# A decoder layer with 64 experts: the experts' token rows gathered in four pieces and turned by VectorE

## The reference

```python
x = x + attention(layernorm(x))            # causal, 16 heads, x is 4 x 1024 x 1024, float32
x = x + cross_mix(layernorm(x), ctx)
h = layernorm(x); probs = softmax(h @ gate.T)          # 64 experts
top_val, top_idx = top_k(probs, 8)                     # 8 experts for each token
# experts chosen only as 5th to 8th are replaced by a similar one (similarity >= 0.5)
for each expert: y = (silu(h[tok] @ Wg.T) * (h[tok] @ Wu.T)) @ Wd.T    # 384 wide
x = x + sum over experts of y * weight
```

## Time and profile before

| | |
|---|---|
| median of 3 runs | 7594.9 us (7593.01 to 7607.1) |
| span of the profiled execution | 7591.9 us |
| TensorE busy, whole span | 93% |
| expert stage, 3601.17 to 7591.9 us: TensorE, DVE, ACT, POOL busy | 3971, 1851, 1636, 1300 us of 3991 |
| DMA engines busy there | 59% |

### The profile page before, as it was taken

The page is one execution under the profiler, slowest core; times in us unless marked ns, Lnnn a source line. Parts: engine busy times, 40 slices in busy tenths (PEclk is TensorE's granted clock), DMA queues, the critical chain, the costliest instruction groups (busy, mean ns, idle before and its releaser), DMA issues.

```text
span 7591.9 us, 118507 instructions
## 1 busy us (share of the span) xinstructions
PE 7089.7 (93%) x37743; PEld 5849.8 (77%) x37744; DVE 3948.7 (52%) x7056; ACT 3419.9 (45%) x6382; POOL 1810.6 (24%) x1602
## 2 busy tenths in 40 slices
PE   7998998998995999992999999999999999999999
PEld 5777777777774787872888888888888888888887
DVE  5666666667664344336454444444444444444444
ACT  4666666666664122211344444444444444444443
POOL 1122122122110000000333333333333333333333
PEclk9999999999997999995999999999999999999999
DMA  2222222222212222221565555665555565566555
GB/s 73 55 66 59 54 65 62 54 64 62 55 50 82 84 64 75 78 70 32 157 182 155 156 159 159 168 180 160 161 163 161 160 166 160 161 163 170 159 158 151
DMA packets 313829, 875.34 MB, mean 115 GB/s; under 512 B 44128, under 2 KB 85600, under 8 KB 313568
## 3 DMA queue, kind: packets, MB, share of 16 engines
q0 software_dynamic: 98928, 365.58, 20.7%
q1 hardware_dynamic: 214640, 506.45, 20.6%
HBM read 614.84 MB, written 206.70 MB: 108 GB/s over the span
## 4 chain that ended last, share of the span: by engine, by line
PE 52%; DVE 0%; DMA 0%; POOL 0%; issue 0%; ACT 0%; DVEq 0%; POOLq 0%; ACTq 0%
PE ps_gu L1928 10%; PE ps_gu L1930 10%; PE ps_gu L1929 10%; PE ps_y L1928 5%; PE ps_y L1930 5%; PE ps_y L1929 5%; PE ps_xe L1948 3%; PE ps_xe L1957 1%; PE ps_l L1937 1%; PE ps_h L2040 0%; DVE logits L2202 0%; DMA out<-y_sup,scatter_s 0%; DMA x_rows<-rows,gather_s 0%; DVE xs_lo L2248 0%; DVE at_hi L2195 0%
## 5 line engine op out<-in xcount | busy, mean ns | idle before, releaser
L1928 PE MATMUL ps_gu<-xs_hi,gu_hi 128*128 128x512 f32 x3072 | 1213.5, 395 | 7.3 <-DVE gu_lo L2287 7.3
L1930 PE MATMUL ps_gu<-xs_hi,gu_lo 128*128 128x512 f32 x3072 | 1207.7, 393 | 0.0
L1929 PE MATMUL ps_gu<-xs_lo,gu_hi 128*128 128x512 f32 x3072 | 1204.8, 392 | 0.0
L1907 POOL TENSOR_TENSOR dn_lo<-raw_w,dn_hi 128x512 fp32r<-128x512 f32 x384 | 485.1, 1300 | 945.3 <-ACT dn_hi L2110 945.3
L1928 PEld LDWEIGHTS ps_gu<-xs_hi,gu_hi 128*128 128x128 f32 x3072 | 578.0, 188 | 130.6 <-DVE gu_lo L2287 7.7
L1929 PEld LDWEIGHTS ps_gu<-xs_lo,gu_hi 128*128 128x128 f32 x3072 | 578.2, 188 | 125.2
L1930 PEld LDWEIGHTS ps_gu<-xs_hi,gu_lo 128*128 128x128 f32 x3072 | 577.7, 188 | 125.0
L454 PE MATMUL ps_qkv<-xt_hi,w_hi 128*128 128x512 f32 x1512 | 619.6, 410 | 17.6 <-ACT proj L610 9.9
L1928 PE MATMUL ps_y<-dn_hi,hs_hi 128*128 128x512 f32 x1536 | 628.6, 409 | 0.1
L889 DVE TENSOR_TENSOR pt_lo<-ps_t,pt_hi 128x512 fp32r<-128x512 f32 (+3 forms) x768 | 425.4, 554 | 376.3 <-ACT pt_hi L710 371.6
L454 PE MATMUL ps_qkv<-xt_lo,w_hi 128*128 128x512 f32 x1512 | 609.7, 403 | 0.0
(11 more groups left out here) (325 smaller groups left out, 15534.7 us busy)
## 6 DMA issues: line engine op xcount, KB each, us to landing
raw_w<-w_gu SPq DMA_DIRECT2D x384, 512.0 KB, 4.1
raw_w<-w_down SPq DMA_DIRECT2D x192, 512.0 KB, 6.5
w_raw<-wqkv SPq DMA_DIRECT2D x192, 256.0 KB, 2.6
turned<-proj SPq DMA_DIRECT2D x512, 64.0 KB, 2.0
out<-residual SPq DMA_DIRECT2D x36, 512.0 KB, 2.6
q_hi<-q_hi SPq DMA_DIRECT2D x128, 128.0 KB, 2.3
attn_out<-out_t POOLq DMA_DIRECT2D x128, 128.0 KB, 2.3
residual<-x SPq DMA_DIRECT2D x32, 512.0 KB, 4.6
```

What stands on the lines that cost most here:

```text
L1907: pool.tensor_tensor(dn_lo[:, f, a], raw_w[:, f, a], raw(dn_hi[:, f, a]), ALU.subtract).then_inc(dn_lo_ok, 1)
L1928: pe.matmul(out, a_hi, w_hi, start=first, stop=False)
L1929: pe.matmul(out, a_hi, w_lo, start=False, stop=False)
L1930: return pe.matmul(out, a_lo, w_hi, start=False, stop=last)
```

## The change

In `rows` a token is now four pieces of 256 features, each followed by 64 columns; the routing weights stand in the first piece, and zeros in the other three. One gather of 128 rows becomes four of 128 pieces: the gather for slot `q` brings pieces such that partitions 32j to 32j+31 hold the j-th quarter of the features of 32 tokens. DVE then turns all 32 x 32 squares of such a block in place with one instruction (`turn_super`, `turn_tail` on DVE), and the features are on partitions. TensorE's turns and `ps_xe` are gone. ACT and DVE split a block with one instruction of 1024 elements instead of two of 512, and DVE's now reads SBUF twice where one input was in PSUM. The host lays the first layer's weights out in the same order of features.

The list of row numbers of an expert is written into one of four slots of a ring (`table`), and 16 further instructions on 32 partitions each write the numbers of the pieces (`pieces`). The three first gathers of an expert's blocks are issued one expert earlier, behind the `send_super` of the same number; the fourth stays where all four were.

```diff
-                sp.dma_start(rows[row:row + P, 0:H], work[:, 1, :]).then_inc(x3_out, 16)
+                sp.dma_start(rows[row:row + P, :, 0:QF], work[:, 1, :].rearrange("p (q c) -> p q c", q=Q4)).then_inc(x3_out, 16)
...
-                sp.dma_start(rows[a, 0:H], res[:, 0, :]).then_inc(zero_out, 16)
-                sp.dma_start(rows[a, H:H + E], res[:, 0, 0:E]).then_inc(zero_out, 16)
+                sp.dma_start(rows[a, :, 0:QF], res[:, 0, :].rearrange("p (q c) -> p q c", q=Q4)).then_inc(zero_out, 16)
                 sp.dma_start(out[a, :], res[:, 0, :]).then_inc(zero_out, 16)
...
+            for q in range(Q4):
+                sp.dma_start(rows[:, q, QF:ROW].rearrange("(n p) e -> p n e", p=P),
+                             blank[:, :].unsqueeze(1).broadcast_to([P, SUP + N, E])).then_inc(blank_out, 16)
...
-        xt_lo = m.sb("xtail_lo", [P, H], F32R)
+        xt_hi = m.sb("xtail_hi", [P, HB, P], F32R)
+        xt_lo = m.sb("xtail_lo", [P, HB, P], F32R)
         act_s = m.sb("act_s", [P, TOKENS])
         hs_hi = m.sb("hs_hi", [P, FB, TOKENS], F32R)
         hs_lo = m.sb("hs_lo", [P, FB, TOKENS], F32R)
@@ -1752,11 +1761,12 @@
...
+            pieces_of_rows = rows.rearrange("n q c -> (n q) c")
             def gather_super(n, i):
-                if i == 0:
-                    pool.wait_ge(gs_ok, START + n + 1)
-                    pool.wait_ge(wn_ok, START + n)
-                    pool.wait_ge(xs_ps, START + n * SUP)
-                    stand_alone(pool, passed)
-                pool.indirect_dma_start(x_rows[:, i, 0:H + E], None, rows,
-                                        bass.IndirectOffsetOnAxis(ap=gather_s[:, i:i + 1], axis=0)).then_inc(rows_s[i], 16)
+                pool.wait_ge(gs_ok, START + n + 1)
+                pool.wait_ge(wn_ok, START + n)
+                if not (isinstance(n, int) and n == 0):
+                    pool.wait_ge(xs_lo_ok, START + (n - 1) * SUP + i + 1)
+                stand_alone(pool, passed)
+                for q in range(Q4):
+                    pool.indirect_dma_start(x_rows[:, i, q, 0:ROW], None, pieces_of_rows,
+                                            bass.IndirectOffsetOnAxis(ap=gather_s[:, i * Q4 + q:i * Q4 + q + 1], axis=0)).then_inc(rows_s[i], 16)
             def gather_tail(n):
                 pool.wait_ge(gt_ok, START + n + 1)
                 pool.wait_ge(wtn_ok, START + n)
-                pool.wait_ge(xt_ps, START + n)
+                pool.wait_ge(xt_lo_ok, START + n)
                 stand_alone(pool, passed)
-                pool.indirect_dma_start(xt_rows[:, 0:H + E], None, rows,
-                                        bass.IndirectOffsetOnAxis(ap=gather_t[:, 0:1], axis=0)).then_inc(rows_t, 16)
+                for q in range(Q4):
+                    pool.indirect_dma_start(xt_rows[:, q, 0:ROW], None, pieces_of_rows,
+                                            bass.IndirectOffsetOnAxis(ap=gather_t[:, q:q + 1], axis=0)).then_inc(rows_t, 16)
...
             for i in range(SUP):
                 gather_super(0, i)
+            for i in range(SUP - 1):
+                gather_super(1, i)
             def super_block(e, t0, t1):
                 send_last(e + t0)
                 gather_tail(e + t0)
-                for i in range(SUP):
-                    gather_super(e + 1, i)
+                gather_super(e + 1, SUP - 1)
                 for n in range(2 * FB):
                     pool.wait_ge(hi_ok, START + e * 2 * CHUNKS + 2 * GUC + n + 1)
                     f, a = n // 2, slice(n % 2 * BANK, (n % 2 + 1) * BANK)
                     pool.tensor_tensor(dn_lo[:, f, a], raw_w[:, f, a], raw(dn_hi[:, f, a]), ALU.subtract).then_inc(dn_lo_ok, 1)
                 for i in range(SUP - 1):
                     send_super(e, t0, i)
-            def tail_block(e, t):
+                    gather_super(e + 2, i)
+            def tail_block(e, t, t0):
                 gather_tail(e + 1 + t)
                 send_last(e + 1 + t)
...
-            def turn_super(n, i, tails):
-                pe.wait_ge(rows_s[i], (n + 1) * 16)
-                pe.wait_ge(xt_lo_ok, START + tails * 2)
-                pe.wait_ge(xs_lo_ok, START + n * 2 * SUP + 2 * i)
-                for k in range(HB):
-                    mm = pe.transpose(ps_x1[:, k * P:(k + 1) * P], x_rows[:, i, k * P:(k + 1) * P], ident[:, :])
-                mm.then_inc(xs_ps, 1)
...
-                turn_tail(e + t0, e + 1)
                 first_layer(2, 0)
                 first_layer(2, 1)
-                turn_super(e + 1, 0, e + 1 + t0)
...
                 for i in range(1, SUP):
-                    turn_super(e + 1, i, e + 1 + t0)
                     for c in range(2):
...
                 turn_h(1)
-                turn_tail(e + 1 + t, e + 2)
                 turn_h(2)
...
             def split_super(n, i):
...
+                act.wait_ge(xs_turned, START + n * SUP + i + 1)
...
                 act.wait_ge(up_ok, START + n * FB)
-                for c in range(2):
-                    ks = slice(c * GQ, (c + 1) * GQ)
-                    act.activation(xs_hi[:, ks, i * P:(i + 1) * P],
-                                   ps_x1[:, c * BANK:(c + 1) * BANK].rearrange("p (k c) -> p k c", c=P), ACT.Copy).then_inc(xs_hi_ok, 1)
+                act.activation(by_feature(xs_hi[:, :, i * P:(i + 1) * P]), in_order(x_rows[:, i, :, :]), ACT.Copy).then_inc(xs_hi_ok, 1)
             def split_tail(n, t):
-                act.wait_ge(xt_ps, START + n + 1)
...
-                    split_super(e + 1, i)
-                    if i < SUP - 1:
-                        finish(i)
-            def tail_block(e, t):
+                split_super(e + 1, 0)
+                split_super(e + 1, 1)
+                finish(0)
+                split_super(e + 1, 2)
+                split_super(e + 1, 3)
+                finish(1)
+                finish(2)
...
-                at = tails_before(dve, n) + n * SUP
-                dve.tensor_tensor(table[:, bass.ds(at + 1, N)], found[:, 0, :], found[:, 1, :], ALU.add).then_inc(list_ok, 1)
+                at = (n & AHEAD) * N
+                dve.tensor_tensor(found[:, 0, :], found[:, 0, :], found[:, 1, :], ALU.add).then_inc(total_ok, 1)
+                dve.wait_ge(total_ok, START + n + 1)
+                stand_alone(dve, passed)
+                dve.tensor_copy(table[:, bass.ds(at, N)], found[:, 0, :])
+                mine = pieces[:, bass.ds(at * Q4, N * Q4)].rearrange("p (n i) -> p n i", i=Q4)
+                for q in range(Q4):
+                    for i in range(Q4):
+                        ins = dve.tensor_scalar(mine[32 * q:32 * q + 32, :, i], found[32 * i:32 * i + 32, 0, :], float(Q4), float(q), ALU.mult, ALU.add)
+                ins.then_inc(list_ok, 1)
...
-                dve.tensor_copy(gather_s[:, :], table[:, bass.ds(n * SUP + tails + 1, SUP)]).then_inc(gs_ok, 1)
+                dve.tensor_copy(gather_s[:, :], pieces[:, bass.ds((n & AHEAD) * N * Q4, SUP * Q4)]).then_inc(gs_ok, 1)
...
+                dve.tensor_copy(gather_t[:, :], pieces[:, bass.ds(at * Q4, Q4)]).then_inc(gt_ok, 1)
+            def turn_super(n, i):
+                dve.wait_ge(rows_s[i], (n + 1) * 64)
+                dve.transpose(x_rows[:, i, :, 0:QF], x_rows[:, i, :, 0:QF]).then_inc(xs_turned, 1)
+            def turn_tail(n):
+                dve.wait_ge(rows_t, LOADED + (n + 1) * 64)
+                dve.transpose(xt_rows[:, :, 0:QF], xt_rows[:, :, 0:QF]).then_inc(xt_turned, 1)
...
             def rest_of_super(n, i):
-                for c in range(2):
-                    dve.wait_ge(xs_hi_ok, START + n * 2 * SUP + 2 * i + c + 1)
-                    a = slice(i * P, (i + 1) * P)
-                    ks = slice(c * GQ, (c + 1) * GQ)
-                    dve.tensor_tensor(xs_lo[:, ks, a], ps_x1[:, c * BANK:(c + 1) * BANK].rearrange("p (k c) -> p k c", c=P),
-                                      raw(xs_hi[:, ks, a]), ALU.subtract).then_inc(xs_lo_ok, 1)
+                dve.wait_ge(xs_hi_ok, START + n * SUP + i + 1)
+                a = slice(i * P, (i + 1) * P)
+                dve.tensor_tensor(by_feature(xs_lo[:, :, a]), in_order(x_rows[:, i, :, :]), raw(by_feature(xs_hi[:, :, a])),
+                                  ALU.subtract).then_inc(xs_lo_ok, 1)
...
-                dve.tensor_copy(w_next[:, :], x_rows[:, :, bass.ds(n + H, 1)].rearrange("p i a -> p (i a)")).then_inc(wn_ok, 1)
+                for i in range(Q4):
+                    ins = dve.tensor_copy(w_next[32 * i:32 * i + 32, :], x_rows[0:32, :, i, bass.ds(n + QF, 1)].rearrange("p s a -> p (s a)"))
+                ins.then_inc(wn_ok, 1)
...
             make_list(0)
             finish_list(0)
-            gather_super_index(0, 0)
+            gather_super_index(0)
             make_list(1)
+            turn_super(0, 0)
+            for i in range(SUP):
+                if i + 1 < SUP:
+                    turn_super(0, i + 1)
+                rest_of_super(0, i)
             keep_weights(0)
```

(19 more changed lines are left out.)

120 lines of the change are left out of this document (58 added, 62 removed).

## The result

The changed kernel takes 8393.8 us (median of 4 runs, 8354.8 to 8417.5), the kernel before 7599.1 us beside it: a ratio of 1.1042 (95% interval 1.1013 to 1.1072), 10% slower. The direction of the forecast was right, its size was not: 7837 was forecast, and 8060 was the upper end.

A forecast was written before the change was run, and what follows sets the result against it. The prediction took TensorE to bound the expert stage (busy 3971 of 3991 us). Its terms, -282 + 179 + 279 + 51 + 15 = +242 on 7591.9, plus 3.0 to the median, gave 7837 us, range 7555 to 8060.

The forecast's parts named there:

- term 3: Tail: POOL's scatters and 12 gathers make the tail's rows late, delaying the next expert's first product; +279 us.
- At nothing: Effects charged zero: mixing-stage stores, ACT's saved instructions, and gathers with 18% more bytes, four times the packets, queues having room.
- Term 1: Transposes removed from TensorE: 320 turns of eight in dense streams at 0.88 us each save 282 us.
- Term 2: Second layer: DVE is 3.2 us late for multiply(2), so TensorE waits 2.8 us in each expert; +179 us.
- The turn: DVE's 128 x 1024 transpose instruction, taken as 1.2 us; a skill-based estimate gave 2.5 us.
- Term 4: End of the second layer: results leave ps_y late, 0.8 us in each of 64 experts; +51 us.
- Term 5: Start: sixteen gathers instead of four ahead of the first expert, and three lists with 16 pieces each; +15 us.
- A gather of pieces is cheap: Faster rival: on POOL, a gather step below 0.71 us removes term 3, 7558 us; deciding point 0.79 us; chance 0.13.
- DVE is later still: Slower rival: DVE's lateness for multiply(2) costs 5.5 us an expert in Term 2, giving 8008 us; chance 0.22.

The follow-up runs named there:

- e1: The changed kernel with one gather of 128 whole rows in place of four gathers of pieces, same bytes, rows not rightly placed: 7780.3 us, ratio 1.0241.
- e3: The changed kernel with DVE's order alone changed: finish_list last in super_block, turn_super(3) behind rest_of_h(2): 7953.5 us, ratio 1.0469.
- e7: The changed kernel with e1 and e3 together, one gather for a block and finish_list last: 7473.9 us, ratio 0.9845.
- e11: The changed kernel with all its work in another order on POOL and DVE, gathers in shorter runs, one finish of ACT moved: 8088.2 us, ratio 1.0651.
- e4: The kernel before with each gather of 128 rows made four gathers of 128 quarter rows at the same place: 8559.4 us, ratio 1.1259.
- e14: e13 with one wait changed: POOL starts the gathers of blocks 1 and 2 when hs_lo of f = 0 is written: 7571.0 us, ratio 0.9969.
- e8: The kernel before with two gathers of half rows in place of each gather, at the same place: 7861.3 us, ratio 1.0348.
- e9: e4 with three of every four gathers replaced by a direct DMA of the same 128 x 1,088 bytes, issued by POOL: 7597.0 us, ratio 1.0002.
- e10: The kernel before with 15 memsets of 128 x 1024 on POOL behind the five gathers, no further DMA: 7595.2 us, ratio 0.9995.
- e13: The changed kernel with all its work, POOL, DVE and ACT reordered, blocks 1 and 2 gathered behind the fifth weight's low parts: 7658.4 us, ratio 1.0095.

## Why the prediction was wrong, step by step

- **The step that failed.** The prediction charged 20 gathers only with POOL's own time (term 3), put nothing for what they do to the other engines, and said under "At nothing" that the queues have room. The room was there (DMA share 0.54), and it was the wrong thing to ask. Gathers in a long run hold up PE, ACT and DVE. First layers: (39.9 - 34.1) x 34 + (37.8 - 34.2) x 30 = 305 us against e1, a term that the sum did not have. Tails: 370 us, under term 3. e1 takes 614 us off the changed kernel with nothing but the number of gathers (305 in the first layers, 319 in the tails).
- **Term 1, -282.** Right where it can be seen: a first layer without gaps is 34.1 us, 1.65 less than before, for two turns (1.76).
- **Term 2, +179.** The mechanism was right and the size too small. DVE took 15.0 us where 14.2 was worked out, and the waits are 231 us instead of 179. What the term left out is the clock: behind each wait TensorE runs at half its clock, 118 us more. Together 349, at the upper end of 350. e3 shows the cause.
- **The turn.** 1.2 us was taken, 1.24 and 1.25 are measured above. The estimate of 2.5 us from the Trainium skill, VectorE: DVE Perf Modes, "The three transpose paths", does not hold for this one 128 x 1024 instruction. The 16 pieces take 3.2 us against 2.7.
- **Term 3, +279.** POOL's own time was right: a step of 1.25 us (0.95 + 0.30) against 1.31, and 26.0 us from the first scatter to the tail's fourth gather (5093.47 to 5119.47) against 31.9 - 6.1 = 25.8. The fourth gather still came 37.0 us after the second layer's start at 5082.45, not 31.9, since the first scatter stood at 11.0 instead of 6.1, behind the wait of term 2, which this term did not count. The place where it costs was wrong. gu_lo costs 17.4 us in all. The same run of gathers already held ACT, DVE and PE up inside the tail, and the tails grew by 30 x 12.35 = 370 us; e1, with the turn on DVE but few gathers, has tails of 16.1. That a term of 279 stood where 370 were measured is luck.
- **Term 4, +51.** 1.6 us: the late second layer hid it. It came back where DVE was on time, with 28.7 us in 62 waits for y_sup in e7 and 21.8 in e3.
- **Term 5, +15.** The first product of the first expert starts at 3623.8 instead of 3608.9 us: 14.8. One execution doesn't tell it so well: e3, whose program is the same up to there, starts at 3634.4.
- **The sum with measured terms** is -282 + 305 + 349 + 370 + 2 + 15 = +759, against +797 between the two spans. Of the rest, 11 us stand at the end of the last expert; 27 are not traced to a place. The direction was right for term 2's sake: with one gather (e1) the change is still 2.4% slower.
- **The rivals.** "A gather of pieces is cheap" fell by its own point, 0.79 us. "DVE is later still" had the right size for term 2 by another way. The rule of the Trainium skill, SBUF — State Buffer, "SBUF: two separate sides", by which a whole instruction keeps the port pair, agrees with found (1.04 and 1.22 us, 0.19 in e3); e11's 8.6 us is more than it says, since six instructions in a row kept DVE out.

What holds the engines back in a run of indexed DMAs is open. The gaps look like missing instructions: they come on PE, ACT and DVE alike, with nothing to wait for, and end when POOL pauses. The Trainium skill, Runtime: NRT & Kernel Launch, "Instruction fetch mechanics", says that each sequencer drives its own DMA queue to fetch its next page. The changed kernel's trace has packets of such a kind, and they do not bear that reading out. These are its queues (packets, MB, share of 16 engines) from 3600 to 3800 us, and then from 3800 to 8388:

```profile
q0 software_dynamic: 4641, 16.23, 35.0%
q1 hardware_dynamic: 3168, 11.54, 17.8%
q8 instruction: 3, 0.05, 0.1%
q14 instruction: 5, 0.04, 0.1%
```

```profile
q0 software_dynamic: 104799, 366.87, 34.9%
q1 hardware_dynamic: 79344, 288.92, 18.9%
```

Eight instruction packets stand in the first passes of the expert loop and none in the rest of it, where nearly all the gaps are; in e4 none stands from 3725 to 8546 us. Whether every engine's fetches are recorded, no run shows, nor why direct DMAs from POOL do no harm. Open is also why dn_lo lets DVE in between its instructions in one order and not in the other. And e14 leaves it open how much of its late second layers a third buffer for y_sup would take away; it wasn't tried.

## What to carry to other kernels

Count indexed DMAs as instructions, not as bytes or rows: 32 rows cost nearly what 128 do. Before splitting one, ask what a long run of them does to the other engines, and look in the trace for idle time without a releaser. If many are needed, break them into short runs with a pause (runs of up to 13 us in e14 left PE 41 us of such idle time in all, e8's 15 us cost 268 us), and keep them off the places where gaps show up in the trace. An engine that gives work to DVE frees its own time only if DVE's program has room at the place where the work lands; and a wait of TensorE that this causes costs more than its length, since the clock is halved behind it: 118 us behind 231 of waiting here.

## What the runs showed of the hardware

- 15 more indexed gathers an expert (and 3 more a tail) in a run cost 961 us (e4), the same number as direct DMAs nothing (e9), and 15 memsets an expert nothing (e10).
- A gather takes 0.95 us with 128 pieces of 1,280 or of 256 bytes, and 0.86 with 32 rows of 4,352.
- A DVE instruction with both inputs in SBUF was held for 7.4 us under six POOL instructions (e11), and a gather took 1.96 instead of 0.95 us beside DVE's work in SBUF (e13).
- A turn of 128 x 1024 in 32 x 32 blocks in place takes 1.24 us; on TensorE it took 0.88.
